# New stage positions in the expert loop of a two-layer transformer, and an indirect-transfer queue without tile marks

## The chip, the cores and the metric

One core of one Trainium2 chip runs the whole program. The metric is the device time of one execution in microseconds (us). Each engine runs its own instruction queue: TensorE (PE), VectorE (DVE), ScalarE (ACT), GpSimd (POOL) and the DMA-issuing SyncE (SP). They meet at semaphores only.

## The reference

The input is x of shape 16 x 512 x 128. Two residual layers follow each other; the time in question is spent in the last part of the second:

```python
x = x + attn0(layernorm(x));  x = x + ffn0(layernorm(x))
x = x + attn1(layernorm(x), ...)                # causal, 16 heads
z = layernorm(x)
for _ in range(2):                              # LOOPS
    zn = rmsnorm(z, norm_w)
    scores = softmax(zn @ router_w)             # 8 experts
    w, idx = top_k(scores, 2);  w = w / (sum(w) + 1e-9)
    mixed = sum over both experts e of a token: w_e * (silu(zn @ w1[e]) * (zn @ w3[e])) @ w2[e]
    z = z + mixed
x = x + z
```

There are 8192 tokens, width 128, hidden width 256, two experts for each token.

## The kernel before

The first part (attention, feed-forward, attention) ends near 1580 us of the profile. What follows is the function experts, and the change lies wholly in it.

**Groups.** The 8192 tokens are cut into 8 groups of 8 x 128 tokens. A group passes the router twice and is then added up once more, so there are 24 sides: k = 0 to 7 are the groups in loop 0, k = 8 to 15 in loop 1, k = 16 to 23 only the final sum. The text says group k for side k. The router work of group 0 is done before this function. For groups 1 to 6 the means and roots are ready beforehand; the code calls such a group made.

**Units and tiles.** Scatter k writes the 1024 normalized rows of group k twice, sorted by expert, into rows_in (16 indirect DMAs of 128 rows, issued by POOL). Groups are taken together in units: unit 0 is group 0, units 1 to 7 are groups 1-2, 3-4, ..., 13-14, unit 8 is group 15. A unit of one group has 23 tiles of 128 rows, a unit of two has 39; there are 319 tiles, and the unit borders lie at tiles 23, 62, 101, 140, 179, 218, 257 and 296. Every tile belongs to one expert. Gather k (16 indirect DMAs by POOL) fetches the expert outputs of group k-8 from rows_out into yg.

**The tile pipeline.** Every engine runs a loop over n with a function tile(n), which holds its part of the pipeline. On PE: transposes of h for tile n-6, the gate-up product for n-2, the down product for n-8, the transpose of the loaded rows for n (L1678; this signals step_done). ACT copies and applies Silu. DVE multiplies h for tile n-2 (L1839) and copies y for tile n-8 (L1848). PE's tile(n+3) waits for the y that DVE's tile(n) copied, since they share a PSUM bank. ACT stores y of tile n-9 to rows_out in its tile(n).

**The sides.** Between tiles each engine does pieces of router work, side(k, s), of stages s = 0 to 20, and s = 21 to 28, the tables of a unit (which rows and which expert each tile has, and where gathers read). What matters below:

- s 0 to 3: add the gathered rows (k of 8 and more), or for group 7 bn statistics and root; s 4: DVE computes z (L1913/L1914, L1930/L1931)
- s 5 and 6: PE transposes z in two halves through one PSUM bank (L1695), ACT copies each (zT, L1752); s 8: router product on PE (L1700); s 9: copy by ACT, xn by DVE; s 10: second half of xn, transposes back on PE
- s 12 to 15: DVE chooses both experts, ending in selb; ACT takes Exp at s 15 (L1759), with a table load before it and another before the next Silu; s 16: PE counts with selb (L1713, L1715)
- s 17, 18: DVE weights; s 19, 20: DVE slots, ending in scat_idx (L1994), which releases scatter k

The place of a stage is set by the dictionary begin and by the function sides: stage s of group k stands behind tile begin[k] + s * length(k) // 21 on DVE, one tile later on ACT and two later on PE (the argument behind of run). The list transfers orders the scatters (s) and gathers (g) on POOL. In front of each of their DMAs the function after_tile can put a wait on a PE tile; the function assigned computes these marks, with half a tile between two DMAs at least. SP loads the rows of tile n when tile n-8 is transposed and, at a unit's first tile, when its scatters have landed (L1623 to L1629).

Of the kernel before, what the change touches and what calls it, by code (L numbers as in the profile page):

```python
# [385 lines left out]
IT = 8  # L386
# [1033 lines left out]
def experts(nc, x, z, w13, w2, w_in, out_done, lead, w, tri, ins, out, rows_in):  # L1420
# [20 lines left out]
    EARLY, PER_TILE = 2, 0.5  # L1441
    begin = {2: -1, 3: 8, 4: 22, 5: 34, 6: 46, 7: 60, 8: 76, 9: 97, 10: 117, 11: 137, 12: 158, 13: 179, 14: 200, 15: 224,
             16: 256, 17: 270, 18: 286, 19: 308, 20: 325}
    transfers = ("s1 s2 s3 g8 s4 s5 s6 g9 s7 g10 s8 g11 s9 g12 s10 g13 s11 g14 s12 g15 s13 g16 s14 g17 s15 g18 "
                 "g19 g20 g21 g22 g23").split()

    def length(k):

        return 10 if k < GROUPS - 1 else 14 if k < GROUPS else 20 if k < LOOPS * GROUPS else 8

    def sides(n):

        return [(k, s) for k, at in begin.items() for s in range(STAGES + TABLES) if at + s * length(k) // STAGES == n]

    def assigned():

        ready, due_at = [], []
        for name in transfers:
            k = int(name[1:])
            if name[0] == "s":  # L1460
                ready += [0 if k < EARLY else begin[k] + (STAGES - 1) * length(k) // STAGES + 1] * (2 * IT)
                due_at += [base_of[unit_of[k]] - RING] * (2 * IT)
            else:
                ready += [base_of[unit_of[k - GROUPS] + 1] + LAG + 1] * (2 * IT)
                due_at += [begin.get(k, N + LAG + 1) - 1] * (2 * IT)
        at, spread = -1.0, []
        for r in ready:
            at = max(r, at + PER_TILE)
            spread.append(int(at))
        latest = N + LAG  # L1470
        for i in range(len(spread) - 1, -1, -1):
            latest = min(latest, due_at[i])
            spread[i] = min(spread[i], latest)
        return spread
# [17 lines left out]
    with ExitStack() as ctx:  # L1492
# [106 lines left out]
        def run(tile, side, behind):  # L1599
# [4 lines left out]
            for n in range(N + LAG + 1 + behind):  # L1604
                tile(n)
                for k, s in sides(n - behind):
                    side(k, s)
# [170 lines left out]
        def _(pool):  # L1778
# [5 lines left out]
            def after_tile(tiles):  # L1784

                at = next(tiles)
                if at > 0:
                    pool.wait_ge(step_done, at)

            def scatter(k, tiles):  # L1790
# [3 lines left out]
                for a in range(2):  # L1794
                    for t in range(IT):
                        after_tile(tiles)
# [4 lines left out]
            def gather(k, tiles):  # L1801
# [21 lines left out]
        def _(dve):  # L1823
# [59 lines left out]
            def side(k, s):  # L1883
# [52 lines left out]
                if not routes(k):  # L1936
                    return
# [224 lines left out]
```

## Time and profile before

| | before |
|---|---|
| median of 3 runs | 2240.81 us (2240.65 to 2243.47) |
| the profiled execution | 2240.62 us, span 2238.8 us |
| PE / DVE / ACT / POOL busy, share of the span | 89% / 82% / 66% / 55% |
| POOL gathers (L1811), whole kernel | 256 DMAs, 250.1 us busy, 977 ns each |
| POOL scatters (L1797) | 240 DMAs, 236.2 us busy, 984 ns each |

The span lies 1.8 us under the execution's own time. Busy shares are means over parts of the program with different limits; the expert loop is read from its own stretch, from 1584 us on. A DMA issue on POOL counts as busy there.

### The profile page before, as it was taken

How to read it: one execution, taken by the hardware profiler on the slowest of the kernel's cores; microseconds unless marked ns; L12 is line 12 of the kernel's file. 1: busy time of each engine (PE TensorE's matmuls, PEld its weight loads, DVE VectorE, ACT ScalarE, POOL GpSimd, SP SyncE). 2: the span in 40 equal slices, each digit the busy share in tenths (PEclk: the TensorE clock that was granted, in tenths of full speed). 3: DMA queues.
4: the chain of work that ended last, by engine and by line, in shares of the span. 5: the costliest groups of instructions: out<-in, count | busy, mean ns of one | idle time of the engine just before them, and what ended most of it. 6: DMA issues, size and time to landing. Idle time of an engine off the chain costs nothing. (4 is left out here: it accounts for less than half of the span.)

```text
span 2238.8 us, 47085 instructions
## 1 busy us (share of the span) xinstructions
PE 1989.0 (89%) x14589; PEld 951.3 (42%) x14589; DVE 1827.6 (82%) x5158; ACT 1467.0 (66%) x3369; POOL 1234.4 (55%) x1708
## 2 busy tenths in 40 slices
PE   5999999999998899889999999997688999999993
PEld 1222222222222366444444444443355666666662
DVE  8899999999999576788888888888677777767555
ACT  1788888888888623477777777773455655565551
POOL 6253343334321002476767677754767777777776
PEclk9999999999999999799999999997799999999996
DMA  7345335444542002234242433322233444444544
GB/s 188 106 118 144 110 105 139 137 105 122 144 106 87 11 1 57 58 69 106 59 113 61 100 75 87 87 60 64 83 108 112 123 121 119 121 127 124 145 136 114
DMA packets 224625, 226.92 MB, mean 101 GB/s; under 512 B 34049, under 2 KB 187521, under 8 KB 224385
## 3 DMA queue, kind: packets, MB, share of 16 engines
q1 hardware_dynamic: 152432, 164.62, 28.5%
q0 software_dynamic: 16384, 33.59, 5.3%
q10 hardware_dynamic: 55568, 25.71, 4.1%
q8 instruction: 126, 2.06, 0.4%
q14 instruction: 115, 0.93, 0.1%
HBM read 96.48 MB, written 125.76 MB: 99 GB/s over the span
## 5 line engine op out<-in xcount | busy, mean ns | idle before, releaser
L937 ACT ACTIVATE big<-mid_ps 128x512 f32<-128x512 f32 (+2 forms) x1792 | 914.2, 568 | 266.1 <-PE mid_ps L816 258.4
L1022 DVE TENSOR_REDUCE mid_nmax<-mid_ps 128x1 f32<-128x512 f32 (+2 forms) x1280 | 776.4, 657 | 61.3 <-PE mid_ps L795 36.2
L795 PE MATMUL mid_ps<-KT,QT 48*128 48x512 bf16 (+3 forms) x2048 | 604.4, 351 | 68.2 <-DVE mid_nmax L1022 49.6
L816 PE MATMUL mid_ps<-QT,KT 64*128 64x512 bf16 (+3 forms) x2048 | 563.9, 346 | 2.6 <-ACT big L937 2.2
L832 PE MATMUL mid_ps<-big,vv 128*32 128x512 f32 (+3 forms) x4096 | 466.7, 529 | 17.0 <-POOL big L1153 13.3
L795 PEld LDWEIGHTS mid_ps<-KT,QT 48*128 48x128 bf16 x2048 | 158.9, 94 | 585.1 <-DVE mid_nmax L1022 397.3
L1019 DVE CUSTOM_DVE_ANT_0 big<-mid_ps,mask 128x512 bf16<-128x512 f32 (+1 forms) x512 | 304.4, 619 | 68.5 <-PE mid_ps L795 63.7
L1666 PE MATMUL moe_ps<-big,moe_xinT 128*128 x638 | 332.1, 602 | 0.0
L1811 POOL DMA_INDIRECT moe_yg<-rows_out,moe_gat_idx x256 | 250.1, 977 | 85.9 <-issue 65.7
L1797 POOL DMA_INDIRECT rows_in<-moe_xn,moe_scat_idx x240 | 236.2, 984 | 81.2 <-issue 61.3
L1839 DVE TENSOR_TENSOR moe_h<-moe_ps,moe_sg 128x256 f32<-128x256 f32 x319 | 135.0, 423 | 157.3 <-ACT moe_sg L1737 152.6
L1728 ACT ACTIVATE moe_xinT<-moe_ps,norm_w 128x128 f32<-128x128 f32 x319 | 116.9, 366 | 221.9 <-PE moe_ps L1678 151.0
L1673 PEld LDWEIGHTS moe_ps<-big,moe_hT 128*128 128x128 f32 x1276 | 192.6, 191 | 150.4 <-issue 150.4
L1153 POOL TENSOR_SCALAR_AFFINE_SELECT big<-big 128x512 f32<-128x512 f32 x256 | 156.9, 643 | 151.8 <-ACT big L937 150.5
L1673 PE MATMUL moe_ps<-big,moe_hT 128*128 x1276 | 194.4, 275 | 0.0
L1137 POOL TENSOR_TENSOR x<-x,mid_ao 128x256 f32<-128x256 f32 x32 | 23.2, 724 | 308.2 <-DVE mid_ao L1038 308.2
L1659 PE MATMUL moe_ps<-ident,moe_h 128*128 128x128 f32 x638 | 126.4, 280 | 32.5 <-DVE moe_y L1848 31.8
L816 PEld LDWEIGHTS mid_ps<-QT,KT 64*128 64x128 bf16 x2048 | 136.1, 94 | 19.9 <-ACT big L937 15.9
L832 PEld LDWEIGHTS mid_ps<-big,vv 128*32 128x32 f32 x4096 | 81.7, 108 | 134.3 <-issue 97.0
L1737 ACT ACTIVATE moe_sg<-moe_ps 128x256 f32<-128x256 f32 x319 | 123.6, 387 | 0.2
L1732 ACT ACTIVATE moe_hT<-moe_ps 128x256 f32<-128x256 f32 x319 | 120.4, 378 | 2.7 <-PE moe_ps L1673 2.0
L1094 POOL TENSOR_TENSOR mcols<-mid_nmax,nought 128x16 bf16<-128x16 f32 x128 | 28.5, 223 | 161.9 <-DVE mid_nmax L1022 161.9
(359 smaller groups left out, 3017.7 us busy)
## 6 DMA issues: line engine op xcount, KB each, us to landing
l_spread<-mid_slots SPq DMA_DIRECT2D x128, 384.0 KB, 5.3
rows_in<-mid_blank SPq DMA_DIRECT2D x64, 512.0 KB, 4.4
QT<-l_spread SPq DMA_DIRECT2D x128, 192.0 KB, 4.3
KT<-l_spread SPq DMA_DIRECT2D x128, 192.0 KB, 5.3
moe_xin<-rows_in SPq DMA_DIRECT2D x319, 64.0 KB
rows_out<-moe_y ACTq DMA_DIRECT2D x319, 64.0 KB
x<-in_L_attn_x_dram SPq DMA_DIRECT2D x8, 512.0 KB, 6.9
QT<-mid_mrows SPq DMA_DIRECT2D x256, 6.0 KB
```

What stands on the lines that cost most here:

```text
L795: mm = pe.matmul(ps[:, bank, n_keys * a:n_keys * (a + 1)], QT[rows, par, pair, i * P:(i + 1) * P], KT[rows, par, pair, 0:n_keys], start=Tr ...
L816: mm = pe.matmul(ps[:, bank, m * a:m * (a + 1)], KT[rows, own, pair, i * P:(i + 1) * P], QT[rows, own, pair, SEQ - m:SEQ], start=True, sto ...
L832: mm = pe.matmul(ps[32 * j:32 * j + 32, O, first(kt):SEQ], vv[:, ((r - 3) // 4) % 2, kt, 4 * ((r - 3) % 4) + j, :], weights_of(r - 3, kt, ...
L937: act.activation(weights_of(r, i, heads), ps[:, ring(S2, n - 2, k), 0:widths[i] * len(heads)], ACT.Exp, scale=scale).then_inc(exp_done, 1)
L1019: dve.tensor_tensor_reduce(thrown[:, (SLOTS * n + k) % len(S1), 0:width(i)], of, w["mask"][:, SEQ - width(i):SEQ], -1.0, 3.0e38, ALU.add, ...
L1022: dve.tensor_reduce(to, of, X_AXIS, ALU.max, negate=True).then_inc(s1_used, 1)
L1153: pool.affine_select(out=diagonal, in_=diagonal, compare_op=ALU.is_ge, fill=0.0, base=0, pattern=[[0, 4], [1, P]], channel_multiplier=-1). ...
L1666: mm = pe.matmul(ps[:, GU[v % BANKS], :], xinT[:, v % 2, :], w13[:, bass.ds(expert(v), 1), :].rearrange("p a f -> p (a f)"), start=True, s ...
L1673: mm = pe.matmul(ps[:, bank, Y:Y + DIM], hT[:, v % 2, c * P:(c + 1) * P], w2[:, bass.ds(e, 1), c, :].rearrange("p a d -> p (a d)"), start= ...
L1797: pool.indirect_dma_start(rows_in[u % CHUNKS], bass.IndirectOffsetOnAxis(ap=scat_idx[:, loop, a, t0 + t:t0 + t + 1], axis=0), xn[:, k % 3, ...
L1811: pool.indirect_dma_start(yg[:, k % 3, a, t, :], None, rows_out[u], bass.IndirectOffsetOnAxis(ap=gat_idx[:, loop, a, t0 + t:t0 + t + 1], a ...
L1839: dve.tensor_tensor(h[:, v % 4, :], ps[:, GU[v % BANKS], FF:2 * FF], sg[:, v % BANKS, :], ALU.mult)\
```

## The change

It gives every stage of a made group a position of its own on each engine, moves the begin values of groups 2 to 7 and 9, spreads the tables of a made group over four tiles, puts ACT's stages 5 and 6 of the other groups one tile later, moves group 1's z (s 4) on DVE ahead of the tables of unit 0, puts scatter 4 ahead of gather 8 and scatter 7 ahead of gather 9, and takes out all tile marks of the indirect transfers.

```diff
@@ -1438,40 +1438,36 @@
     word_of = [sum(words_in[:u]) for u in range(UNITS + 1)]
     HT, MOST = IT * max(sizes), max(tiles_in)
     unit_of = [max(u for u in range(UNITS) if first_of[u] <= k) for k in range(LOOPS * GROUPS)]
-    EARLY, PER_TILE = 2, 0.5
-    begin = {2: -1, 3: 8, 4: 22, 5: 34, 6: 46, 7: 60, 8: 76, 9: 97, 10: 117, 11: 137, 12: 158, 13: 179, 14: 200, 15: 224,
+    EARLY = 2
+    begin = {2: -2, 3: 7, 4: 18, 5: 33, 6: 44, 7: 56, 8: 76, 9: 98, 10: 117, 11: 137, 12: 158, 13: 179, 14: 200, 15: 224,
              16: 256, 17: 270, 18: 286, 19: 308, 20: 325}
-    transfers = ("s1 s2 s3 g8 s4 s5 s6 g9 s7 g10 s8 g11 s9 g12 s10 g13 s11 g14 s12 g15 s13 g16 s14 g17 s15 g18 "
+    transfers = ("s1 s2 s3 s4 g8 s5 s6 s7 g9 g10 s8 g11 s9 g12 s10 g13 s11 g14 s12 g15 s13 g16 s14 g17 s15 g18 "
                  "g19 g20 g21 g22 g23").split()
 
     def length(k):
 
-        return 10 if k < GROUPS - 1 else 14 if k < GROUPS else 20 if k < LOOPS * GROUPS else 8
-
-    def sides(n):
-
-        return [(k, s) for k, at in begin.items() for s in range(STAGES + TABLES) if at + s * length(k) // STAGES == n]
-
-    def assigned():
-
-        ready, due_at = [], []
-        for name in transfers:
-            k = int(name[1:])
-            if name[0] == "s":
-                ready += [0 if k < EARLY else begin[k] + (STAGES - 1) * length(k) // STAGES + 1] * (2 * IT)
-                due_at += [base_of[unit_of[k]] - RING] * (2 * IT)
-            else:
-                ready += [base_of[unit_of[k - GROUPS] + 1] + LAG + 1] * (2 * IT)
-                due_at += [begin.get(k, N + LAG + 1) - 1] * (2 * IT)
-        at, spread = -1.0, []
-        for r in ready:
-            at = max(r, at + PER_TILE)
-            spread.append(int(at))
-        latest = N + LAG
-        for i in range(len(spread) - 1, -1, -1):
-            latest = min(latest, due_at[i])
-            spread[i] = min(spread[i], latest)
-        return spread
+        return 14 if k < GROUPS else 20 if k < LOOPS * GROUPS else 8
+
+    ON_PE, ON_ACT, ON_DVE = 2, 1, 0
+    AHEAD = {ON_PE: {5: 0, 6: 1, 8: 2, 10: 3, 16: 6}, ON_ACT: {5: 1, 6: 2, 9: 3, 15: 6},
+             ON_DVE: {4: 0, 9: 2, 10: 3, 12: 5, 13: 6, 14: 6, 15: 7, 19: 8, 20: 8, 17: 9, 18: 9}}
+
+    def tile_of(k, s, behind):
+
+        if made(k) and s < STAGES:
+            return max(begin[k] + AHEAD[behind].get(s, 0), -behind)
+        if made(k):
+            return begin[k] + 10 + (s - STAGES) // 2
+        late = 1 if behind == ON_ACT and s in (5, 6) and routes(k) else 0
+        return begin[k] + s * length(k) // STAGES + late
+
+    def sides(n, behind):
+
+        return [(k, s) for k in begin for s in range(STAGES + TABLES) if tile_of(k, s, behind) == n - behind]
+
+    def made(k):
+
+        return 1 <= k < GROUPS - 1
 
     def routes(k):
 
@@ -1603,7 +1599,7 @@
                     side(k, s)
             for n in range(N + LAG + 1 + behind):
                 tile(n)
-                for k, s in sides(n - behind):
+                for k, s in sides(n, behind):
                     side(k, s)
             for k in range(EARLY + len(begin), SIDES):
                 for s in range(STAGES + TABLES):
@@ -1781,24 +1777,17 @@
             for i in range(lead.SENT, 2 * IT):
                 lead.scatter(pool, i)
 
-            def after_tile(tiles):
-
-                at = next(tiles)
-                if at > 0:
-                    pool.wait_ge(step_done, at)
-
-            def scatter(k, tiles):
+            def scatter(k):
                 loop, t0, u = k // GROUPS, tiles_of(k), unit_of[k]
                 pool.wait_ge(xn_ready, k + 1)
                 pool.wait_ge(scat_ready, k + 1)
                 for a in range(2):
                     for t in range(IT):
-                        after_tile(tiles)
                         pool.indirect_dma_start(rows_in[u % CHUNKS],
                                                 bass.IndirectOffsetOnAxis(ap=scat_idx[:, loop, a, t0 + t:t0 + t + 1], axis=0),
                                                 xn[:, k % 3, t, :], None).then_inc(scattered[k % 3], 16)
 
-            def gather(k, tiles):
+            def gather(k):
                 loop, t0, u = k // GROUPS - 1, tiles_of(k), unit_of[k - GROUPS]
                 pool.wait_ge(tables, u + 1)
                 for s in range(RING):
@@ -1807,17 +1796,15 @@
                     pool.wait_ge(added, k - GROUPS - 2)
                 for a in range(2):
                     for t in range(IT):
-                        after_tile(tiles)
                         pool.indirect_dma_start(yg[:, k % 3, a, t, :], None, rows_out[u],
                                                 bass.IndirectOffsetOnAxis(ap=gat_idx[:, loop, a, t0 + t:t0 + t + 1], axis=0))\
                             .then_inc(last_rows[2 * a + 2 * t // IT] if k == SIDES - 1 else gathered[k % 3], 16)
 
-            tiles = iter(assigned())
             for name in transfers:
                 if name[0] == "s":
-                    scatter(int(name[1:]), tiles)
+                    scatter(int(name[1:]))
                 else:
-                    gather(int(name[1:]), tiles)
+                    gather(int(name[1:]))
 
         @block.vector
         def _(dve):
@@ -1907,7 +1894,7 @@
                         moments()
                         c.link(dve.tensor_tensor(ms[:, :], mean[:, :], mean[:, :], ALU.mult))
                         c.link(dve.scalar_tensor_tensor(var[:, :], var[:, :], 1e-6, ms[:, :], ALU.add, ALU.add))
-                elif 1 <= k < GROUPS - 1:
+                elif made(k):
                     own = slice(IT * (k - 1), IT * k)
                     if s == 4:
                         c.link(dve.tensor_tensor(zs, xs, each_row(lead.means[:, own]), ALU.subtract))
@@ -1933,17 +1920,19 @@
                     if s == 5:
                         c.link(dve.tensor_tensor(var[:, :], var[:, :], rstd[:, :], ALU.mult))
                         c.link(dve.tensor_scalar(var[:, :], var[:, :], 1e-6, None, ALU.add))
+                if (k, s) == (1, 5):
+                    for part in range(TABLES):
+                        make_tables(0, part)
                 if not routes(k):
                     return
 
-                made = 1 <= k < GROUPS - 1
-                scale = lead.scales[:, IT * (k - 1):IT * k] if made else rstd[:, :]
-                if s == 6 and not made:
+                scale = lead.scales[:, IT * (k - 1):IT * k] if made(k) else rstd[:, :]
+                if s == 6 and not made(k):
                     rsqrt_seed(c, rstd[:, :], var[:, :])
                     cubic_root(c, rstd[:, :], var[:, :], tmp[:, :])
-                if s == 7 and not made:
+                if s == 7 and not made(k):
                     cubic_step(c, rstd[:, :], tmp[:, :])
-                if s == 8 and not made:
+                if s == 8 and not made(k):
                     c.link(newton(c, rstd[:, :], var[:, :], tmp[:, :]))
                 if s in (9, 10):
                     if s == 9 and k >= 3:
@@ -2053,8 +2042,6 @@
                     else:
                         c.link(last)
 
-            for part in range(TABLES):
-                make_tables(0, part)
             run(tile, side, 0)
```

For a made group the stages now stand behind these tiles, counted from begin[k]: DVE 0 (s 4), 2 and 3 (xn), 5, 6, 6, 7 (choice), 8 (s 19, 20), 9 (s 17, 18), 10 to 13 (tables); ACT 2, 3, 4 and 7 (Exp); PE 2, 3 (transposes of z), 4, 5, 8 (counts). Before, DVE computed z behind begin[k]+1 and PE transposed both halves behind begin[k]+4.

The queue of POOL, before. A row is one or more batches of 16 indirect DMAs in a row; L1797 and L1811 are scatter and gather, rows_in2 holds unit 2 (groups 3 and 4), rows_in3 unit 3 (5 and 6), rows_in0 unit 4 (7 and 8).

```order
L1797 DMA rows_in1<-moe_xn,moe_scat_idx 16384x128 x32
L1797 DMA rows_in2<-moe_xn,moe_scat_idx 16384x128 x16
L1811 DMA moe_yg<-rows_out0,moe_gat_idx 128x128 x16
L1797 DMA rows_in2<-moe_xn,moe_scat_idx 16384x128 x16
L1797 DMA rows_in3<-moe_xn,moe_scat_idx 16384x128 x32
L1811 DMA moe_yg<-rows_out1,moe_gat_idx 128x128 x16
L1797 DMA rows_in0<-moe_xn,moe_scat_idx 16384x128 x16
```

The same place of the changed kernel, where the two lines are L1786 (scatter) and L1799 (gather).

```order
L1786 DMA rows_in1<-moe_xn,moe_scat_idx 16384x128 x32
L1786 DMA rows_in2<-moe_xn,moe_scat_idx 16384x128 x32
L1799 DMA moe_yg<-rows_out0,moe_gat_idx 128x128 x16
L1786 DMA rows_in3<-moe_xn,moe_scat_idx 16384x128 x32
L1786 DMA rows_in0<-moe_xn,moe_scat_idx 16384x128 x16
L1799 DMA moe_yg<-rows_out1,moe_gat_idx 128x128 x32
```

Scatter 4 now goes ahead of gather 8, and scatter 7 ahead of gathers 9 and 10.

DVE before, where unit 3's tables end and group 7 begins (h and y are the tile's own work, moved and gat_idx the last table parts, stats the bn statistics of group 7).

```order
L1839 TENSOR_TENSOR moe_h<-moe_ps,moe_sg 128x256
L1848 COPY moe_y<-moe_ps 128x128
L2046 TENSOR_TENSOR moe_moved<-moe_keep_sel,moe_move 128x128
L2047 TENSOR_REDUCE moe_moved_by<-moe_moved 128x16
L2048 TENSOR_TENSOR moe_gat_idx<-moe_keep_at,moe_moved_by 128x2x8
L1839 TENSOR_TENSOR moe_h<-moe_ps,moe_sg 128x256
L1848 COPY moe_y<-moe_ps 128x128
L1870 BN_STATS moe_stats<-x 128x6 x8
```

The changed kernel at the same work, behind tile 56.

```order
L1826 TENSOR_TENSOR moe_h<-moe_ps,moe_sg 128x256
L1835 COPY moe_y<-moe_ps 128x128
L2017 TENSOR_TENSOR moe_tab<-moe_iota_f,moe_tab 1x39
...
L2024 TENSOR_TENSOR moe_row_of<-moe_tab 1x39
...
L2029 CAST moe_words<-moe_sums 1x5
L1857 BN_STATS moe_stats<-x 128x6 x8
...
L1826 TENSOR_TENSOR moe_h<-moe_ps,moe_sg 128x256
L1835 COPY moe_y<-moe_ps 128x128
L2035 TENSOR_TENSOR moe_moved<-moe_keep_sel,moe_move 128x128
```

Group 7's statistics now share a tile with parts 4 and 5 of unit 3's tables, and the last table parts come after them.

## Rows read from the trace of the kernel before

**Rows 1.** The page: the span.

```profile
span 2238.8 us, 47085 instructions
```

**Rows 2.** POOL's groups from 1740 to 2234 us: busy, mean, idle before.

```profile
L1811 POOL DMA_INDIRECT moe_yg<-rows_out,moe_gat_idx x240 | 234.4, 977 | 77.2 <-issue 61.4 <-PE moe_ps L1678 9.8 <-DMA rows_out<-moe_y 4.5
L1797 POOL DMA_INDIRECT rows_in<-moe_xn,moe_scat_idx x144 | 140.7, 977 | 43.9 <-issue 33.6 <-PE moe_ps L1678 9.1 <-DMA rows_out<-moe_y 1.2
```

**Rows 3.** POOL's timeline: first DMA of scatters 1 and 3, gathers 8, 9, 21.

```profile
1584.47 1.32 POOL L1797 DMA_INDIRECT rows_in<-moe_xn,moe_scat_idx  x1 [4.67 <-DVE moe_scat_idx L1994]
...
1629.83 0.97 POOL L1797 DMA_INDIRECT rows_in<-moe_xn,moe_scat_idx  x1 [3.93 <-issue]
...
1654.11 0.99 POOL L1811 DMA_INDIRECT moe_yg<-rows_out,moe_gat_idx  x1 [4.14 <-DMA rows_out<-moe_y]
...
1740.86 0.98 POOL L1811 DMA_INDIRECT moe_yg<-rows_out,moe_gat_idx  x1 [3.93 <-DMA rows_out<-moe_y]
...
2171.29 0.95 POOL L1811 DMA_INDIRECT moe_yg<-rows_out,moe_gat_idx  x1 [0.61 <-issue]
```

**Rows 4.** ACT's queue, timeline: the store of tile 295, unit 7's last.

```profile
2168.50 0.33 ACTq L1743 DMA_DIRECT2D rows_out<-moe_y  x1
```

**Rows 5.** The chain that ended last, near its end: start, us, what.

```profile
2232.29 2.52 DMA moe_yg<-rows_out,moe_gat_idx
```

**Rows 6.** PE's tile transposes, from tile 0 on: count, durations, first and last start.

```profile
L1678 PE MATMUL moe_ps<-ident,moe_xin x52: 272/273/475, 1584.2 to 1695.8; 128*128 128x128 f32 x52
L1678 PE MATMUL moe_ps<-ident,moe_xin x70: 272/273/475, 1584.2 to 1735.6; 128*128 128x128 f32 x70
L1678 PE MATMUL moe_ps<-ident,moe_xin x77: 272/273/475, 1584.2 to 1748.0; 128*128 128x128 f32 x77
```

**Rows 7.** PE's timeline where group 3's z is transposed: wait ahead in brackets.

```profile
1609.74 0.74 PE L1695 MATMUL moe_ps<-ident,big 128*128 128x128 f32 x4 [3.21 <-DVE big L1914]
```

**Rows 8.** One stretch: length, busy (count) of each engine, PE's granted clock, DMA, GB/s.

```profile
1610.00:1618.00 8.00, 6.85 (x29) 3.95 (x28) 7.26 (x28) 3.48 (x9) 6.17 (x7) 0.57 0.28 85
```

**Rows 9.** DVE's timeline: both parts of z of group 3; tables and statistics, 1709 to 1719 us.

```profile
1607.20 1.23 DVE L1913 TENSOR_TENSOR big<-x,lead_means 128x1024 f32<-128x1024 f32 x1
1608.46 1.22 DVE L1914 TENSOR_TENSOR big<-big,lead_roots 128x1024 f32<-128x1024 f32 x1
...
1709.32 0.22 DVE L2010 TENSOR_SCALAR moe_full<-moe_iota_f 128x128 f32<-128x128 f32 x1
...
1718.22 0.42 DVE L1839 TENSOR_TENSOR moe_h<-moe_ps,moe_sg 128x256 f32<-128x256 f32 x1
...
1718.76 1.63 DVE L1870 BATCH_NORM_STATS2 moe_stats<-x 128x6 f32<-128x128 f32 x8
```

**Rows 10.** PE's and DVE's timelines around Exp of group 7: tile 71, h of tile(72), slots.

```profile
1738.86 0.27 PE L1678 MATMUL moe_ps<-ident,moe_xin 128*128 128x128 f32 x1
...
1744.08 0.42 DVE L1839 TENSOR_TENSOR moe_h<-moe_ps,moe_sg 128x256 f32<-128x256 f32 x1 [1.73 <-ACT moe_sg L1737]
...
1746.91 0.17 DVE L1994 CAST moe_scat_idx<-moe_keep_at 128x16 int32<-128x16 f32 x1
```

**Rows 11.** PE and DVE timelines: an undelayed tile; DVE's selb of group 4.

```profile
1634.67 0.27 PE L1678 MATMUL moe_ps<-ident,moe_xin 128*128 128x128 f32 x1
1636.30 0.27 PE L1678 MATMUL moe_ps<-ident,moe_xin 128*128 128x128 f32 x1
...
1636.27 0.28 DVE L1848 COPY moe_y<-moe_ps 128x128 f32<-128x128 f32 x1
...
1650.31 0.22 DVE L1972 TENSOR_TENSOR moe_selb<-moe_keep_sel 128x64 bf16<-128x64 f32 x1
```

**Rows 12.** DVE's timeline: group 1's z, its logits and scat_idx; PE's tile 0.

```profile
1568.79 1.22 DVE L1913 TENSOR_TENSOR big<-x,lead_means 128x1024 f32<-128x1024 f32 x1
...
1577.70 0.22 DVE L1960 TENSOR_TENSOR moe_lg<-moe_ps,lead_scales 128x64 f32<-128x64 f32 x1 [5.09 <-PE moe_ps L1709]
...
1584.18 0.45 PE L1678 MATMUL moe_ps<-ident,moe_xin 128*128 128x128 f32 x1 [2.49 <-DMA moe_xin<-rows_in]
```

## The prediction

> **What bounds the kernel now.** I read the page, then POOL's groups and timeline over the expert loop, then the timelines of PE, DVE and ACT side by side, then the end of the chain. The profiled execution took 2240.62 us with a span of 2238.8 [rows 1], so 1.8 us lie around the span; it is 0.2 under the median.
>
> Two chains set the end, and both are full. The first is POOL's queue. From 1740.86 to its last gather it shows no wait longer than its issue gap: 240 gathers and 144 scatters, 977 ns each and about 0.3 us between two, so 16 of them cost 20.3 to 20.4 us [rows 2]. Its last gather lands at 2234.8 [rows 5]. Ahead of 1740.86 it waited four times: 4.67 us for scat_idx of group 1, 3.93 at scatter 3, 4.14 at gather 8 and 3.93 at gather 9, the last two for stores of unit 0 and unit 1 [rows 3]. The second chain is the pace of the tiles. Gather 21 needs all of unit 7, so the store of tile 295, which ACT issued at 2168.50 [rows 4]; gather 21 began 2.8 us later, after 0.61 instead of 0.3 us [rows 3]. So a shorter queue alone brings only 0.3 us at the end, and faster tiles alone bring 0.3 at most too. What counts is the smaller lead of the two.
>
> **Tile times.** T(n) is the start of the transpose of tile n, by counting: T(0) 1584.2, T(51) 1695.8, T(69) 1735.6, T(76) 1748.0 [rows 6]. Undisturbed tiles are 1.63 us apart, and DVE is done with tile(n) 1.9 us after T(n) [rows 11]. Since PE's tile(n+3) needs DVE's tile(n), DVE may be late by only 1.4 us; after that a tile costs what DVE does in it: 0.54 for h and y plus the side. From T(0) to T(76) the plain pitch would give 124 us, and 163.8 were taken. Of the 40 us about 18 are PE's own router work and Exp's table loads; some 22 are waits, like the 3.21 us for z of group 3 [rows 7]. These are what the new stage tables can save.
>
> DVE's prices, from the distance of starts: z 2.5 us, group 7's statistics 1.63 and with its moments 2.8, a unit's eight table parts 7.3 (8.9 from 1709.32 to 1718.22, less three tiles of 0.54) [rows 9]. From the same timeline xn takes 0.65 twice, the choice 3.3 over three tiles, s 17 and 18 1.3, s 19 and 20 1.45.
>
> **The change part by part.**
>
> Tile marks. A DMA behind a mark that had long been reached shows the same 0.3 us gap as the others (9.8 us for the gathers released by PE, all in such gaps) [rows 2]. Removing them: 0, and at most the 0.3 at gather 21.
>
> Group 1's z ahead of the tables. z begins at 1568.79 after 5.7 us of tables and the logits come 8.9 us after z begins, after a wait of 5.09 for PE and ACT [rows 12]. The tables now fill that wait, so scat_idx comes about 5 us sooner and scatter 1 starts when scatter 0 is through, 4.4 us sooner. Tile 0 does not gain: it waits for its rows [rows 12], which need scatter 0 alone.
>
> Scatter 4 ahead of gather 8, scatter 7 ahead of gather 9. The waits at both gathers go, if the scatters are ready. I follow POOL: scatter 1 at 1580.1, scatter 2 at 1601.1 (group 2's slots then just ready, at 1600.7), scatter 3 at 1624.5, scatter 4 at 1648.1, gather 8 at 1668.7, scatters 5 and 6, done at 1731.3. Then scatter 7 must wait for its slots. Until then the queue is some 10 us ahead; whether it keeps that hangs on this one wait, and that on the tiles.
>
> Stage tables, tiles 0 to 21. Group 2's z is ready at 1581.2 and its router work goes into the filling of the pipeline. But its slots are behind tile 6 and its weights and group 3's z behind tile 7: 1600.7 + 0.4 + 1.3 + 2.5 gives 1604.9 for z, and PE, which wants it behind tile 9, is there at 1601.8. That is a wait of 3 us in the place of 3.21. Then DVE has seven tiles (3.8 us) with tables, xn and choice (12 us) to do until selb of group 3, 1620.7, where PE waits again, as s 16 now stands one tile behind s 15 instead of two. T(16) becomes 1622.6, and T(21) 1632, against 1631.4.
>
> Groups 4 to 6. A new wait for each z: z is ready 1.9 + 2.5 = 4.4 us after T(begin), and PE asks for it behind tile begin+2, at 3.4: 1.0 us, in the place of about 1.1 us for ACT's copy between the two halves. A new wait for each selb: 1.9 + 1.2 = 3.1 after tile begin+7, PE asks at 1.7: 1.4 us, half of it hidden by the waits that follow Exp anyway. For group 5 tables no longer stand in front of z; that gives 2 us back. The sum is T(51) 1695.0, against 1695.8, with group 6's work as far along as before.
>
> Unit 3's tables and group 7. Begin moves from 60 to 56, and 44 stands for group 6 in the place of 46, so two tiles fewer lie between. DVE's sides behind tiles 52 to 58 are 1.45, 1.3, 1.7, 1.9, 4.8, 2.4 and 3.7. From h behind Exp at 1700.8 the chain gives y of tiles 57, 58, 59 at 1714.5, 1717.5, 1721.7; PE waits 3.6 us ahead of tile 60 and z comes at 1721.2. PE goes on with T(62) 1723.6, T(67) 1733.2. Group 7's slots are written 8.2 us after the tile of Exp (1738.86 to 1747.08) [rows 10], so at 1741.4, and POOL starts 0.8 us after that, as at scatter 1: 1742.2. Then scatter 7, gather 9 and gather 10 follow, as many DMAs as gather 9, scatter 7 and gather 10 before, which started at 1740.86. **The queue's lead is gone, and it is 1.3 us behind.**
>
> The clock. After the wait of 3.21 us ahead of group 3's z the granted clock was 0.57 from 1610 to 1618 [rows 8], half of the time or more at 1.2 GHz. The waits of 3.0 and 3.6 us above are of that length; none is shown in between. The price lies between 0 and 4 us each (8 us at half speed). The first is hidden by the wait for selb; for the second I take 1 us, since DVE holds the next tiles anyway. The Trainium skill, TensorE: Matmul & The Clock Gate (Part 1: The HAM clock gate), says that the default state is throttled and that activity releases it, with K at 4/8 or 8/8 only. By that rule both waits would fall to half rate, which the trace leaves open.
>
> Group 9 one tile later. DVE is full there with unit 4's tables and the adds; one more tile between them saves about 0.8 us of T, behind scatter 7. ACT's stages 5 and 6 one tile later: DVE shows no gap for ACT there, so 0.
>
> **The sum.** Queue: 1.3 + 1.0 later, less the 0.3 of gather 21: 2.0. Tiles: T(76) 1748.9 + 1.0 against 1748.0, less 0.8: 1.1 later. The later one sets gather 21, and the 62 us behind it are unchanged. 2240.6 + 2.0 + 0.2 to the median gives **2243 us**. A change under 0.2% (4.5 us) can't be told from none by this measurement.
>
> **The rivals.** (a) The queue keeps its lead. If neither scatter 7 nor the stores of unit 7 hold it, the saving is 4.4 at scatter 1 and 3.6 at each of three waits: 15.2 us, 2225. It needs Exp of group 7 by tile time 1717 and tile 295 15 us sooner, which is most of the 22 us of waits. 7%. (b) The new waits for z and selb are covered. They are six, 1.0 to 1.4 us, 7 us together; with them gone both chains are 5 to 8 us shorter: 2236. Against it stand the fixed distances of one and two tiles. 12%. (c) Slower: the clock falls at both long waits and isn't hidden. With 8 us at half speed each costs 4 us instead of 0 and 1: 2250. It decides when PE, not DVE, is last in the tiles behind the wait; for it speaks 0.57 behind the only wait of this length. 20%. (d) The forecast, 2238 to 2246: 61%.
>
> **How the numbers follow.** Faster by over 0.2%: (a), (b) and none of (d), 0.19. Slower: (c) and the upper edge of (d), 0.24. The same: 0.57. The range of 2234 to 2249 leaves out (a) and the far side of (c); the forecast's own range is 2238 to 2246.
>
> **What would show it.** Right: POOL's first wait over 1 us behind gather 8 is ahead of scatter 7, with its release from scat_idx at 1741 to 1744; gather 21 starts within 3 us of 2173; PE waits for DVE ahead of tile 10 and tile 60, and for selb in groups 3 to 6; T(51) is within 2 us of 1695. Wrong: scatter 7 starts before 1735, or T(76) is under 1742; then DVE's sides between tiles 7 and 59 were cheaper than their sum here, or ran in gaps that I filled with waits.

## The result, and the profile after

The changed kernel takes 2258.39 us (median of 6 runs, 2256.71 to 2260.95), the kernel before on the same chip 2241.56 us (6 runs, 2240.65 to 2243.95). The ratio is 1.0074, 95% interval 1.0061 to 1.0087: slower by 16.8 us. The forecast was 2243, the range ended at 2249.

The page of the changed kernel gives the span; [rows 1] is its counterpart:

```profile
span 2254.9 us, 47081 instructions
```

Where do the 16.1 us of span arise? The transposes of the loaded rows, counted from tile 0, with their first and last start, are the milestones (the first x is the count, the one at the end of the line counts one form alone). The changed kernel at tiles 76 and 304:

```profile
L1674 PE MATMUL moe_ps<-ident,moe_xin x77: 272/273/446, 1584.5 to 1751.2; 128*128 128x128 f32 x77
L1674 PE MATMUL moe_ps<-ident,moe_xin x305: 272/273/446, 1584.5 to 2184.4; 128*128 128x128 f32 x153
```

The same count to tile 304 in the kernel before:

```profile
L1678 PE MATMUL moe_ps<-ident,moe_xin x305: 272/273/475, 1584.2 to 2168.2; 128*128 128x128 f32 x153
```

Tile 76 is 3.2 us later than in [rows 6], tile 304 is 16.2 later. So **3.2 us were lost up to tile 76, where nearly all of the change lies, and 13.0 between tiles 76 and 304**, the stretch for which the prediction had a gain of 0.8. Behind tile 304 the two kernels need 70.5 and 70.6 us. All times at a tile are from one profiled execution each, and the first tile of an execution can start a few us earlier or later; where that matters below, the distance from tile 0 is given too.

POOL's queue confirms that the tiles, not the queue, set the end. The first DMAs of scatter 7 and of gather 21, POOL's timeline of the changed kernel:

```profile
1744.49 0.96 POOL L1786 DMA_INDIRECT rows_in<-moe_xn,moe_scat_idx  x1 [9.93 <-DVE moe_scat_idx L1983]
...
2187.08 0.95 POOL L1799 DMA_INDIRECT moe_yg<-rows_out,moe_gat_idx  x1 [11.52 <-DMA rows_out<-moe_y]
```

Before, gather 21 had waited 0.61 us [rows 3]. Now the queue is there 11 us ahead of unit 7's stores, though it lost 9.93 us at scatter 7.

What held the tiles back? PE's waits by what they waited for, 1584 to 2215 us, of the changed kernel (total, times, longest):

```profile
PE moe_ps L1655 <- DVE moe_y L1835: 28.6, 35, 3.4
PE moe_ps L1691 <- ACT moe_zT L1748: 13.7, 10, 2.3
PE moe_ps L1709 <- DVE moe_selb L1961: 8.9, 5, 2.4
```

and of the kernel before:

```profile
PE moe_ps L1659 <- DVE moe_y L1848: 31.8, 42, 1.8
PE moe_ps L1695 <- ACT moe_zT L1752: 5.2, 5, 1.2
...
PE moe_ps L1713 <- DVE moe_selb L1972: 0.5, 1, 0.5
```

Two waits between the tiles have grown: selb from 0.5 to 8.9 us (groups 2 to 6, so ahead of tile 76), and zT from 5.2 to 13.7. (The wait for the loaded rows, xin, has grown as well, from 3.0 to 8.5 us in total, but its 8.5 us lie ahead of tile 0, which starts only 0.3 us later.) Cut to the stretch behind 1745 us, PE's group of the transposes of z (busy and mean, then idle ahead) reads in the changed kernel:

```profile
L1691 PE MATMUL moe_ps<-ident,big 128*128 128x128 f32 x56 | 8.6, 276 | 11.4 <-ACT moe_zT L1748 11.4
...
L1691 PE MATMUL moe_ps<-ident,lead_z 128*128 128x128 f32 x8 | 1.2, 276 | 1.3 <-ACT moe_zT L1748 1.3
```

and in the kernel before:

```profile
L1695 PE MATMUL moe_ps<-ident,big 128*128 128x128 f32 x56 | 8.4, 273 | 0.0
```

The first line is groups 9 to 15, from 0.0 to 11.4 us; the second is group 8, whose z lies in another buffer (lead_z), 1.3 us and 0.0 before. So PE waits 12.7 us for zT where 13.0 were lost, and the only stages moved here, besides group 9's begin, are ones 5 and 6, one tile later. Group 8 shows how it works. PE's timeline of the changed kernel:

```profile
1761.32 0.38 PE L1691 MATMUL moe_ps<-ident,lead_z 128*128 128x128 f32 x2
...
1763.06 0.27 PE L1674 MATMUL moe_ps<-ident,moe_xin 128*128 128x128 f32 x1
1764.63 0.63 PE L1691 MATMUL moe_ps<-ident,lead_z 128*128 128x128 f32 x4 [1.30 <-ACT moe_zT L1748]
...
1766.62 0.27 PE L1674 MATMUL moe_ps<-ident,moe_xin 128*128 128x128 f32 x1
```

ACT's, with the store of a tile (L1739, on its queue) and zT (L1748):

```profile
1762.30 0.39 ACT L1733 ACTIVATE moe_sg<-moe_ps 128x256 f32<-128x256 f32 x1
1763.37 0.33 ACTq L1739 DMA_DIRECT2D rows_out<-moe_y  x1
1763.80 0.69 ACT L1748 ACTIVATE moe_zT<-moe_ps,norm_w 128x512 f32<-128x512 f32 x1 [1.11 <-DVE moe_y L1835]
```

and DVE's:

```profile
1763.06 0.28 DVE L1835 COPY moe_y<-moe_ps 128x128 f32<-128x128 f32 x1
```

Follow it backwards. PE's second half of z goes into the one PSUM bank that holds the first half, so it waits until ACT's copy zT has emptied that bank. The copy had had its input since 1761.7, but ACT takes its instructions in order, and ahead of zT stands the store of its tile(n), which needs a y that DVE copies only at 1763.06. Where the copy stood before the change, behind tile(n-1), the last store ahead of it is one tile older, and its y is there. PE may otherwise run three tiles ahead of DVE; through this chain it may not. The step from one tile transpose to the next is 3.56 us here (1763.06 to 1766.62). In the kernel before, the same step, with the same half of z in it, took 2.07 (1757.82 to 1759.89): 1.5 us less. Before, ACT's zT at this place waited for PE's transposes and not for y:

```profile
1758.18 0.36 ACTq L1743 DMA_DIRECT2D rows_out<-moe_y  x1
1758.64 0.69 ACT L1752 ACTIVATE moe_zT<-moe_ps,norm_w 128x512 f32<-128x512 f32 x1 [1.22 <-PE moe_ps L1695]
```

### The profile page after: what moved, and what is told of

Its sections match the earlier page's. It is cut to its first block and busy times, and to the rows that moved or that the text cites. A ratio compares the mean times of both kernels' runs of the same rounds, so it can differ in the third digit from the quotient of the medians.

```text
span 2254.9 us, 47081 instructions
## 1 busy us (share of the span) xinstructions
PE 1992.9 (88%) x14589; PEld 954.3 (42%) x14589; DVE 1827.9 (81%) x5158; ACT 1466.8 (65%) x3369; POOL 1239.2 (55%) x1708
## 5 line engine op out<-in xcount | busy, mean ns | idle before, releaser
L1799 POOL DMA_INDIRECT moe_yg<-rows_out,moe_gat_idx x256 | 251.1, 981 | 89.3 <-issue 76.9
L1786 POOL DMA_INDIRECT rows_in<-moe_xn,moe_scat_idx x240 | 239.7, 999 | 89.0 <-issue 71.4
```

The costliest lines, as they stand in the source:

```text
L1786: pool.indirect_dma_start(rows_in[u % CHUNKS], bass.IndirectOffsetOnAxis(ap=scat_idx[:, loop, a, t0 + t:t0 + t + 1], axis=0), xn[:, k % 3, ...
L1799: pool.indirect_dma_start(yg[:, k % 3, a, t, :], None, rows_out[u], bass.IndirectOffsetOnAxis(ap=gat_idx[:, loop, a, t0 + t:t0 + t + 1], a ...
```

## The experiments

All ratios are to the kernel before, run on the same chip in the same batch (medians 2241.85 us for experiments 1 to 4, 2241.05 for 6 to 9, 2242.51 for 5 and 10 to 12). "g21" is the start of gather 21.

### 1. ACT not late

The changed kernel, with ACT's stages 5 and 6 of groups 7 to 15 where they were.

```diff
-        late = 1 if behind == ON_ACT and s in (5, 6) and routes(k) else 0
-        return begin[k] + s * length(k) // STAGES + late
+        return begin[k] + s * length(k) // STAGES
```

> The changed kernel with one thing undone: ACT's stages 5 and 6 of groups 7 to 15 stand where they stood before. Theory A (the later position puts ACT's copy of z behind the next tile's store, which waits for DVE's y, and PE waits for that copy): from tile 76 on the tile times run as in the kernel before, about 3 us late; the tile chain loses its 13 us, and POOL's queue sets the end. Scatter 7 starts near 1744.5, gather 21 near 2174.5, time 2244 us (ratio 1.0015). PE's waits for zT behind 1745 us: 0. Theory B (the new stage tables of groups 2 to 7 and 9 leave the pipeline out of step for good) and theory C (the free-running indirect DMAs slow loads or stores): 2257 us as the changed kernel, with tile 304 near 2184.

Measured: 2246.36 us (10 runs), ratio 1.0022 (1.0012 to 1.0031), where 2244 was expected. The transposes of the rows up to tile 304, and the transposes of z behind 1745 us:

```profile
L1673 PE MATMUL moe_ps<-ident,moe_xin x305: 272/273/447, 1585.8 to 2170.7; 128*128 128x128 f32 x153
```

```profile
L1690 PE MATMUL moe_ps<-ident,big 128*128 128x128 f32 x56 | 8.4, 273 | 0.0
```

The wait is gone, and the ratio falls from 1.0074 to 1.0022, some 11.7 us. POOL's timeline; g21 is the second line:

```profile
2173.47 0.95 POOL L1798 DMA_INDIRECT moe_yg<-rows_out,moe_gat_idx  x1 [0.30 <-issue]
2174.73 0.95 POOL L1798 DMA_INDIRECT moe_yg<-rows_out,moe_gat_idx  x1 [0.30 <-issue]
```

No gap: with the tiles back, the queue is what ends last, 3.4 us later than in [rows 3]. This is the case that the prediction described: counted between tiles 76 and 304, the changed kernel takes 433.2 us, this one 420.2 and the kernel before 420.2.

### 2. The kernel before, with ACT late alone

```diff
-        return [(k, s) for k, at in begin.items() for s in range(STAGES + TABLES) if at + s * length(k) // STAGES == n]
+        def late(k, s):
+            return 1 if behind == 1 and s in (5, 6) and GROUPS - 1 <= k < LOOPS * GROUPS else 0
+
+        return [(k, s) for k, at in begin.items() for s in range(STAGES + TABLES)
+                if at + s * length(k) // STAGES + late(k, s) == n]
```

> The kernel before with that one thing added: ACT's stages 5 and 6 of groups 7 to 15 one tile later, all else as before. Theory A: the tiles lose about 13 us between tiles 76 and 240 and perhaps 1 us at group 7, gather 21 waits for the store of tile 295 near 2184, time 2254 us (ratio 1.006). Theories B and C: no change, 2241 us.

Measured: 2254.01 us (4 runs), ratio 1.0058 (1.0041 to 1.0075). The rows to tile 304, and z behind 1745 us:

```profile
L1682 PE MATMUL moe_ps<-ident,moe_xin x305: 272/273/476, 1584.5 to 2180.9; 128*128 128x128 f32 x153
```

```profile
L1699 PE MATMUL moe_ps<-ident,big 128*128 128x128 f32 x56 | 8.6, 276 | 11.4 <-ACT moe_zT L1756 11.4
```

One edit alone brings the same 11.4 us of wait and puts tile 304 12.7 us later. Taken out of the change (11.7 us of time) or put into the kernel before (13.0 by the ratio, 0.58% of 2241.85, and 12.2 between the medians), it is worth 12 to 13 us.

### 3. The changed kernel, with ACT's store behind its sides

If the store in front of zT is the cause, moving the store must cure the wait without moving zT.

```diff
-        def run(tile, side, behind):
+        def run(tile, side, behind, last=None):
...
+                if last:
+                    last(n)
...
+            def store(n):
...
-            run(tile, side, 1)
+            run(tile, side, 1, store)
```

> The changed kernel, with ACT's store of y moved behind ACT's side stages of the same tile; the stages 5 and 6 stay one tile late. If the wait of the store for DVE's y is what holds the copy (theory A), the copy starts some 1 us sooner, PE's waits for zT behind 1745 us fall from about 11 us to under 4, and the time is 2244 to 2248 us. If the later position alone is too late whatever stands in front of it, nothing changes: 2256 to 2258 us.

Measured: 2249.8 us (5 runs), ratio 1.0037 (1.0023 to 1.0051), a little over what was expected. Behind 1745 us:

```profile
L1664 PE MATMUL moe_ps<-big,moe_xinT 128*128 x494 | 255.6, 599 | 1.4 <-ACT moe_xinT L1726 1.4
...
L1693 PE MATMUL moe_ps<-ident,big 128*128 128x128 f32 x56 | 8.6, 276 | 0.6
```

PE no longer waits for zT, which shows that the store in front of it was the blocker. Tile 304 comes at 2174.6, 9.8 us sooner than in the changed kernel but 3.9 later than without the late stages. Between tiles 76 and 304 it takes 424.5 us, so 8.7 of the 13.0 us come back and 4.3 don't. Part of that lies in the new place of the store, which still waits for y, now ahead of ACT's next tile (PE shows 1.4 us for xinT); the rest isn't explained.

### 4. The new transfer order without marks, on the old stages

```diff
-    transfers = ("s1 s2 s3 g8 s4 s5 s6 g9 s7 g10 ...
+    transfers = ("s1 s2 s3 s4 g8 s5 s6 s7 g9 g10 ...
...
-                at = next(tiles)
-                if at > 0:
-                    pool.wait_ge(step_done, at)
+                next(tiles)
```

> The kernel before with the new order of scatters and gathers and without tile marks, with the old stages. Theory A with the two chains: tile times as before (tile 304 at 2168), scatter 7 waits for its slots at 1747.1 and starts at 1747.9, gather 21 near 2178, time 2247 us (ratio 1.003); it waits ahead of gather 8 no more. Theory C: tile 304 comes 5 us or more later, time 2252 us or more. If the queue were not a bound at all: 2241.

Measured: 2250.46 us (4 runs), ratio 1.0042 (1.0025 to 1.0059). POOL at scatter 7:

```profile
1748.78 0.96 POOL L1795 DMA_INDIRECT rows_in<-moe_xn,moe_scat_idx  x1 [7.10 <-DVE moe_scat_idx L1992]
```

The order alone loses what the queue had in hand. Scatter 4 waits 6.91 us for its slots (it starts at 1657.68, where gather 8 started at 1654.11 before) and scatter 7 waits 7.10, and g21, in an unbroken queue, at 2179.86 instead of 2171.29. The earlier stages of the change bring scatter 7 to 1744.49, 4.3 us sooner, which does not pay it back. The expectation of 2247 was 3 us short, and it named no wait at scatter 4.

### 5. The marks alone

The kernel before with only the second half of that edit.

> The kernel before without the tile marks of the indirect transfers, and with nothing else changed. The theory (marks cost nothing at this rate, since POOL meets mostly semaphores that are already set, and the transfers behind them are bound by the queue or by stores): tile 304 at 2168 as before, 2240 to 2243 us. The rival (the marks kept the queue from putting 16 transfers at once beside the tiles' own loads and stores): tiles 1 to 5 us later, 2243 to 2247 us.

Measured: 2242.86 us (11 runs), ratio 1.0004 (0.9995 to 1.0013). The marks are worth nothing that can be measured, as the prediction had it.

### 6. Group 1's z ahead of the tables, alone

```diff
+                if (k, s) == (1, 5):
+                    for part in range(TABLES):
+                        make_tables(0, part)
...
-            for part in range(TABLES):
-                make_tables(0, part)
```

> The kernel before with one thing added: group 1's z ahead of the tables of unit 0. By the two chains scatter 1 starts near 1580.5 instead of 1584.5, but gathers 8, 9 and 21 wait for stores that come no sooner, so the 4 us are waited away: tile 304 at 2168, gather 21 at 2171, time 2241 to 2242 us, no change. If POOL's queue alone set the end: 2237 to 2238 us.

Measured: 2243.05 us (10 runs), ratio 1.0009 (1.0000 to 1.0019). Nothing gained. In the profiled execution the whole loop began some 4 us late (tile 0 at 1588.3), so only distances are to be compared. Scatter 1 stands directly behind scatter 0, with a gap of 0.30 us instead of 4.67 [rows 3], and two DMAs later a mark holds it:

```profile
1584.29 0.96 POOL L1797 DMA_INDIRECT rows_in<-moe_xn,moe_scat_idx  x1 [0.30 <-issue]
1585.56 0.96 POOL L1797 DMA_INDIRECT rows_in<-moe_xn,moe_scat_idx  x1 [0.30 <-issue]
1589.05 0.96 POOL L1797 DMA_INDIRECT rows_in<-moe_xn,moe_scat_idx  x1 [2.53 <-PE moe_ps L1678]
```

So this edit gives its lead to a mark, and marks are free only while the queue isn't ahead. A lead at scatter 1 would in any case meet the three waits behind it, at scatter 3, gather 8 and gather 9 [rows 3]; what it is worth without marks was not tested alone.

### 7 and 8. Fewer waits for selb, and weights in Exp's gap

Both on the kernel of experiment 1. First DVE's weights (s 17, 18) two tiles earlier, into the gap that Exp's table loads leave; then also PE's counts (s 16) one tile later, with the slots behind them.

```diff
-             ON_DVE: {..., 15: 7, 19: 8, 20: 8, 17: 9, 18: 9}}
+             ON_DVE: {..., 15: 7, 17: 7, 18: 7, 19: 8, 20: 8}}
```

> The changed kernel with ACT's stages 5 and 6 where they were before (as in the run e1), and with DVE's weights (stages 17 and 18) of the made groups behind tile begin+7, in the gap that DVE has while ACT loads its tables for Exp and Silu, as before the change, instead of behind begin+9. Theory D (the early loss comes from work put on DVE where DVE sets the pace): 1.3 us less after Exp in groups 2, 4 and 6, tile 76 at 1747 to 1749 instead of 1750.5, scatter 7 one or two us sooner than 1743.8, time 2243 to 2245 us where e1 took 2246.4. Rival (the gap is full with stage 15): no difference to e1.

Measured: 2241.97 us (10 runs), ratio 1.0003 (0.9994 to 1.0013), better than the 2243 to 2245 expected, with tile 76 at 1748.4 instead of 1750.5 (162.3 us behind tile 0 instead of 164.7).

```diff
-    AHEAD = {ON_PE: {5: 0, 6: 1, 8: 2, 10: 3, 16: 6}, ...
-             ON_DVE: {..., 15: 7, 17: 7, 18: 7, 19: 8, 20: 8}}
+    AHEAD = {ON_PE: {5: 0, 6: 1, 8: 2, 10: 3, 16: 7}, ...
+             ON_DVE: {..., 15: 7, 17: 7, 18: 7, 19: 9, 20: 9}}
```

> As e5, and PE's counts (stage 16) one tile later, two tiles behind stage 15 as before the change, with DVE's slots (19, 20) one tile later. PE's five waits for selb (8.9 us in e1) shrink to under 1 us. Theory D, where these waits cost time of the tiles: no half-clock stretch ahead of tile 60, tile 76 at 1745 to 1747, time 2240 to 2243 us. Rival (they only stand in for waits that Exp's gap makes anyway): tile 76 as in e5.

Measured: 2238.86 us (10 runs), ratio 0.9992 (0.9982 to 1.0002), tile 76 at 1744.6 (159.2 behind tile 0). PE's waits for selb and for z (big, which DVE writes) are now

```profile
PE moe_ps L1690 <- DVE big L1900: 5.4, 4, 2.8
PE moe_ps L1708 <- DVE moe_selb L1960: 1.3, 2, 0.8
```

In experiment 7 they were 9.0 us for selb, in five places, and 2.6 for z. So 7.7 us of waits for selb were taken away, 2.8 came back as waits for z, and tile 76 comes 3.8 us sooner (1748.4 to 1744.6), 3.1 counted from tile 0.

### 9. Group 7 spread as before, gather 9 ahead of scatter 7

The kernel of experiment 1 with begin 46 and 60 for groups 6 and 7 and the old place of gather 9.

> As e1, with begin of groups 6 and 7 at 46 and 60 again and gather 9 ahead of scatter 7 again. My step on group 7 (its statistics in the same tiles as unit 3's tables make PE wait over 3 us and fall to half clock): the wait of 3.4 us ahead of tile 60 is gone, tile 76 at 1747 to 1749, slots of group 7 near 1747, gather 9 near 1741, time 2241 to 2244 us. If the early tables up to tile 44 are the loss instead, tile 76 stays at 1750 or later and the time at 2245 or more.

Measured: 2243.44 us (10 runs), ratio 1.0008 (0.9999 to 1.0018). The longest wait for y falls from 3.4 to 1.8 us. The queue doesn't idle ahead of scatter 7 any more, but waits 7.78 us for stores ahead of gather 9; g21 at 2174.3 waits for stores as well, with tile 76 at 1748.5. Two things were changed at once, and the interval overlaps that of experiment 1, so no gain is shown for either alone.

### 10 to 12. Towards a faster kernel

On the kernel of experiment 8: gather 9 ahead of scatter 7; the transposes of z one tile later on PE and ACT; and both.

```diff
-    AHEAD = {ON_PE: {5: 0, 6: 1, 8: 2, 10: 3, 16: 7}, ON_ACT: {5: 1, 6: 2, 9: 3, 15: 6},
+    AHEAD = {ON_PE: {5: 1, 6: 2, 8: 3, 10: 4, 16: 7}, ON_ACT: {5: 2, 6: 3, 9: 4, 15: 6},
```

> The version with ACT not late, the weights and the counts of made groups later, and gather 9 ahead of scatter 7. The queue no longer idles 5 us ahead of scatter 7 for its slots, so it has 5 us of lead at gather 21. If the queue was what ended that version, it comes 1 to 3 us under it, 2236 to 2238 us. If its end was set by the stores of unit 7 (gather 21 stood 3.1 us behind tile 304 there, as in the kernel before), nothing is gained: 2238 to 2240 us. I hold the second likelier.

> The version with ACT not late, weights and counts later, and the transposes of z (and all that follows up to the transposes of xn) one tile later on PE and ACT. PE waited 5.4 us in four places for zT there, 2.8 us in the longest. If these waits are on the path of the tiles, tile 76 comes 1.5 to 3 us sooner than 1744.6 and the time is 2235 to 2238 us. If the tile pipeline catches up behind them, or DVE then waits for logits that come a tile later, it stays at 2238 to 2241 us.

> Both of the last two edits: transposes of z one tile later, and gather 9 ahead of scatter 7. If tiles come sooner, the queue must have the lead to use it, which only this version gives: 2234 to 2237 us. If the tiles gain nothing, as the version with gather 9 first, 2237 to 2240 us.

Measured: gather 9 first 2240.87 us (11 runs), ratio 0.9994 (0.9985 to 1.0003), no gain over experiment 8. Its trace shows why:

```profile
1741.18 0.98 POOL L1798 DMA_INDIRECT moe_yg<-rows_out,moe_gat_idx  x1 [6.50 <-DMA rows_out<-moe_y]
```

Gather 9 has no lead to give, since it waits for the stores of unit 1; it starts 153.4 us behind tile 0, and in experiment 8 scatter 7 starts 152.5 behind it. So this run doesn't decide whether the queue or the tiles set the end of experiment 8.

With z later the kernel takes **2235.43 us** (7 runs), ratio 0.9969 (0.9958 to 0.9981). Both together take 2237.09 us (11 runs), ratio 0.9976 (0.9967 to 0.9985), which can't be told from z later alone; there gather 9 waits 3.21 us for stores.

The expectation of z later calls the 5.4 us of waits that it aims at waits for zT; the rows of experiment 8 show them as waits for z itself. Its forecast of a tile 76 sooner by 1.5 to 3 us holds all the same (3.1, or 3.9 counted from tile 0), as does that of the time. The kernel with z later beats both kernels of this case, the one before by 7 us:

```profile
span 2235.0 us, 47080 instructions
```

Its PE waits for z (big), zT and selb, 1584 to 2215 us:

```profile
PE moe_ps L1695 <- ACT moe_zT L1747: 2.0, 2, 1.3
PE moe_ps L1690 <- ACT moe_zT L1747: 1.7, 1, 1.7
PE moe_ps L1690 <- DVE big L1900: 1.1, 1, 1.1
PE moe_ps L1708 <- DVE moe_selb L1960: 1.1, 2, 0.7
```

5.9 us together, where the changed kernel has 26 and the one before 11.6. Tile 76 comes at 1741.5 and g21, 0.34 us behind the DMA before it, at 2166.50: 6.5 and 4.8 us sooner than before. The longest wait left between tiles is 3.3 us for y ahead of tile 60, the crowd of unit 3's tables and group 7.

## Why the prediction was wrong, by its steps

**ACT's stages 5 and 6 one tile later: the step that failed.** The prediction said "DVE shows no gap for ACT there, so 0". It looked at the consumer that matters least. The bank that the copy zT empties is wanted by PE's second half; the question was what stands ahead of zT on ACT after the move, which is one more store with its wait for y. That cost is shown from both sides (experiments 1 and 2) and its mechanism by moving the store (experiment 3): 12 to 13 us for the eight groups behind tile 76, about 1.5 each. No rival held this case either; rival (c), the slower one, looked for its price in the clock.

**Scatter 4 ahead of gather 8, scatter 7 ahead of gather 9.** Right in kind and nearly in size. Scatter 1 started at 1580.5 (forecast 1580.1), scatter 4 at 1650.6 (1648.1), scatter 7 at 1744.5 (1742.2), released by scat_idx as said, after a wait of 9.93 us where the prediction had the queue some 10 us ahead. "The queue's lead is gone, and it is 1.3 us behind" became 2.9 at scatter 7 and 3.4 at gather 21 in experiment 1, without the late stages. Scatter 7 starts at 1743.8 there, 1.6 us over the forecast and 2.9 behind gather 9 of [rows 3]; another 0.5 is lost on the way to gather 21. That is the mis-sized term, and it is what separates experiment 1 from the forecast: its ratio, on the median before, gives 2245.7 against 2243. (The "62 us" behind gather 21 are 63.5 from its start to the last landing, by [rows 3] and [rows 5]; no sum uses them.)

**Stage tables, tiles 0 to 21.** T(21) was forecast at 1632 and came at 1634.8. A wait of 3 us for z of group 3 was forecast; it was 0.85. DVE reached z sooner, and the time went into selb instead: 1.94 us for group 2, which the prediction did not have, and 2.41 for group 3.

**Groups 4 to 6.** T(51) is 1697.1 for 1695.0, just outside the 2 us that were to show the forecast right. The waits for z, forecast at 1.0, are four with 1.0 at the longest, 3.4 us together. Those for selb were forecast at 1.4 each with half of it hidden; they are 8.9 us in five. Experiments 7 and 8 show that they weren't hidden: PE's s 16 one tile later, with the weights out of the way, brings tile 76 from 1750.5 to 1744.6 (from 164.7 to 159.2 us behind tile 0). Rival (b) had the right lever, 5 to 8 us for covered waits; the change as made doesn't pull it.

**Unit 3's tables and group 7.** PE waited 3.45 us ahead of tile 60, forecast 3.6; T(60) is 1719.6.

**The clock.** One fall was priced, at 1 us, behind the wait at tile 60; it came (0.50 from 1716 to 1720). The one ahead of tile 10 did not, as the wait there was 0.85 us; instead two came behind waits of 1.94 and 2.41 us for selb, to which the prediction gave no fall. T(76) was forecast at 1749.9 and is 1751.2. The second of the two falls did not come in experiment 1, whose program is the same up to there: tiles 16 to 21 took 9.6 us in it and 11.0 in the changed kernel. So this one fall cost some 1.4 us, as much as T(76) was missed by; how the other falls and the waits for selb share in T(76) was not measured.

**Marks 0, and tile 0 without gain:** both right (experiment 5; tile 0 at 1584.5). **Group 9 one tile later saves about 0.8:** from tile 92 to 112 experiment 1 takes 40.2 us and the kernel before 40.8; but from tile 76 to 304 both take 420.2, so it is given back.

## What to carry to other kernels

When a step is moved on an engine that also issues DMAs, list what then stands ahead of it on that engine and what each of those waits for; a store that waits for a late producer delays all that follows it, and a buffer with one copy passes the delay on to the other engines. A step that is shifted by one place in every round costs its wait in every round: here eight times 1.5 us made up some 12 of the 16.8 us by which the kernel became slower. And a queue's lead is kept only if no single release in the middle of it comes late, so the order of transfers has to be chosen by the latest release, not by who could go first.

## What the runs showed of the hardware that was not expected

PE's clock fell behind waits much shorter than the 3.21 us of [rows 7]. The changed kernel waits 1.94 us for selb, works 1 to 1.5 us at full rate and then runs at half; likewise behind 2.41 us. PE's timeline (start, duration; a pair of products with xinT takes 1.02 us at full rate and 1.9 at half) and the stretches (the number behind POOL's is the granted clock):

```profile
1598.46 0.21 PE L1709 MATMUL moe_ps<-moe_selb,lead_upper 128*128 128x72 bf16 x1 [1.94 <-DVE moe_selb L1961]
...
1598.97 1.58 PE L1662 MATMUL moe_ps<-big,moe_xinT 128*128 x2
...
1600.98 1.89 PE L1662 MATMUL moe_ps<-big,moe_xinT 128*128 x2
...
1621.72 0.21 PE L1709 MATMUL moe_ps<-moe_selb,lead_upper 128*128 128x72 bf16 x1 [2.41 <-DVE moe_selb L1961]
...
1624.47 1.91 PE L1662 MATMUL moe_ps<-big,moe_xinT 128*128 x2
```

```profile
1600.00:1604.00 4.00, 4.00 (x15) 2.39 (x14) 3.56 (x15) 1.45 (x6) 1.80 (x3) 0.66 0.15 42
...
1623.20:1626.00 2.80, 2.80 (x10) 1.95 (x9) 2.20 (x11) 0.91 (x3) 1.19 (x2) 0.50 0.26 76
```

Nor does the length of the wait decide it. In experiment 1, whose program is the same up to this place, PE waits 2.42 us for the same selb at 1623.01 and keeps its clock:

```profile
1623.01 0.21 PE L1708 MATMUL moe_ps<-moe_selb,lead_upper 128*128 128x72 bf16 x1 [2.42 <-DVE moe_selb L1960]
...
1623.51 1.02 PE L1661 MATMUL moe_ps<-big,moe_xinT 128*128 x2
```

```profile
1620.00:1628.00 8.00, 5.58 (x41) 3.91 (x40) 6.17 (x29) 5.90 (x14) 5.04 (x6) 1.00 0.26 77
```

A second pair: the adds of group 17 on DVE make PE wait for y by the same amount in the kernel before and in the fastest one. The kernel before waits 1.85 us at 2115.21 and keeps its clock:

```profile
2115.21 0.44 PE L1659 MATMUL moe_ps<-ident,moe_h 128*128 128x128 f32 x2 [1.85 <-DVE moe_y L1848]
```

```profile
2114.00:2118.00 4.00, 2.79 (x13) 1.85 (x14) 3.20 (x13) 1.33 (x6) 3.08 (x4) 1.00 0.51 139
```

The one with z later waits 1.86 us at 2109.01 and falls to half:

```profile
2109.01 0.44 PE L1654 MATMUL moe_ps<-ident,moe_h 128*128 128x128 f32 x2 [1.86 <-DVE moe_y L1834]
```

```profile
2109.00:2112.40 3.40, 3.39 (x12) 2.35 (x13) 2.24 (x8) 1.12 (x4) 2.69 (x3) 0.57 0.61 172
```

So the same wait at another moment can leave the clock alone or bring about 3 us at 1.2 GHz, by an estimate from the second pair some 1.5 us of PE's work (3.4 us at 0.57). An edit that only shifts the program by a few us may gain or lose that, and as the first pair shows, two executions can differ by it where their program is the same. The Trainium skill, TensorE: Matmul & The Clock Gate (Part 1: The HAM clock gate), has the two levels and says that how busy the engine has been sets the clock; the traces here agree with the levels, 0.50 and 1.00.
